# A graph layer with seven relations on one core: second batch's order by hand, first layer norm by halves, the turn of the sums moved, the last c products grouped

## The chip, the cores and the metric

One NeuronCore of a Trainium2 chip. The metric is the device time of one launch in microseconds. Beside TensorE (PE, matrix products) the core has VectorE (DVE), ScalarE (ACT) and GpSimd (POOL) for work on elements, and SyncE (SP), whose queue issues the DMA transfers. Each engine runs its own instructions in order; semaphores tie them together.

## What is computed

Sixteen graphs of 512 nodes with 128 features; `adj` is a full 512 x 512 f32 matrix of each. Cut to what matters:

```python
def _L0_gnn_ref(features, A1, A2, W, W_edges, b):
    eye = jnp.zeros_like(A1) + jnp.eye(N, dtype=A1.dtype)
    shifted = jnp.roll(eye, 1, axis=0)              # the roll is over the batch axis
    A_fwd = [A1, A2, shifted]
    A_list = A_fwd + [jnp.swapaxes(a, 1, 2) for a in A_fwd]
    A_list.append(eye)
    A = jnp.stack(A_list, axis=0)
    HW = jnp.einsum('bnf,rfo->rbno', features, W[:, :F]) \
        + jnp.einsum('rd,rdo->ro', W_edges, W[:, F:])[:, None, None, :]
    AHW = jnp.einsum('rbnm,rbmo->rbno', A, HW)
    return jnp.max(AHW, axis=0) + b

h = jnp.maximum(_layernorm(x, axis=-1), 0.0)
x = x + _L0_gnn_ref(h, adj, adj, L0_gnn_W, L0_gnn_W_edges, L0_gnn_b)
```

So there are seven products of which three are with h itself (relations 2, 5, 6), two with adjT h (3, 4) and two with adj h (0, 1). The constant c_r of a relation (from W_edges) is added plainly in the first three and times the row or column sum of adj in the other four.

## The kernel before

**Tiles.** Everything is kept turned, features on the partitions and nodes along the free axis, so each result is a 128 x 512 tile in one of the eight PSUM banks. `adj` and `adjT` of a batch come as two 1 MB transfers into one of two buffers each. Products are made in fp32r from a high and a low part: `hi*hi + hi*lo + lo*hi`, three matmuls for one. Of the four 128-row chunks of adj, one (WHOLE) is multiplied in f32 and three (SPLIT) from `a_hi` (ScalarE) and `a_lo` (two chunks by VectorE, the last one by GpSimd); the same for adjT with `aT_hi` and `aT_lo`.

**Stages of a batch b on TensorE**, one after the other (L809 to L819):

- `aggregate_T(b)`: h times adj into bank_gT (L704 to L716),
- `turn_h(b)`: four transposes of h into bank_p1 (L671),
- `turn_sums(b)`: four small matmuls that turn the row and column sums of adj, split into `sum_parts` by GpSimd, into bank_p2 (L679),
- `aggregate(b)`: h times adjT into bank_g (L725 to L736),
- products 0 to 2 with hT (L761 to L763), then `begin_products`: the sums times c into the banks of products 3 to 6 (L751), then products 3 to 6 with gT and g.

**The other engines.** ScalarE makes `a_hi`, `aT_hi` with the sums as their accumulators (`split_adj`, `split_adjT`, L389 to L405), h from x with the scale and shift of the layer norm (`make_h`, L418), the high parts of hT, gT and g, `sumsT` (L446), and the first of the seven maxima (`begin_best`, L453). VectorE does the layer norm's statistics (`variance`, L510 to L517, then `scale_and_shift`, L526 to L528), the low parts (`a_lo` L535, `aT_lo` L542, `h_lo` L548, hT, gT, g), and six maxima `take_best(b, 1..6)` (L576, L579) straight from PSUM. GpSimd makes the last chunks of `a_lo` and `aT_lo`, `sum_parts`, `x_bias` = x + b (L307), and the final sum into `o_sb` (L315).

**What sets the order.** Every engine's queue is written out by hand, a start for batch 0 and a loop over the rest; there is no scheduler. VectorE works ahead: in batch b it does the statistics of batch b+2 and shift and `a_lo` of batch b+1. An instruction that waits holds all behind it on its engine. These waits matter below: `aggregate(b)` writes bank_g, which product 6 of the batch before filled, so it waits for `best_done` of all six maxima of batch b-1 (`pe.wait_ge(best_done, b * NBEST)`); product 2 uses bank_p2, so it waits for `sumsT_ready`; `variance(b)` waits for x of batch b to land (`x_in`); GpSimd's `split_adj_last(b + 1)` waits for `h_lo`. The sync queue issues x, adj, adjT, W, bias and xT in one fixed order (L249 on); its load of adj b+2 waits for `gT_psum` and `a_lo` of batch b.

**The start.** Ten warm-up matmuls, then the turn of h of batch 0, for which x comes in two halves whose statistics are made as one group, then the aggregations of batch 0 in f32, chunk by chunk as the quarters of adj and adjT land.

## Time and profile before

| | before |
|---|---|
| timed runs, median (lowest to highest) | 216.88 us (216.61 to 218.16) |
| profiled execution, its time | 216.98 us |
| profiled execution, its span | 215.3 us |
| TensorE busy | 206.3 us, 96% of the span |
| VectorE, ScalarE, GpSimd busy | 177.0, 160.8, 95.9 us |
| DMA moved | 47.14 MB, mean 219 GB/s |
| mean granted TensorE clock | 0.989 |

The span runs from the first to the last instruction in the trace, the time of an execution also holds what lies around it. All times in the views count from the span's start. "PEclk" is the share of full TensorE clock that was granted. A timeline row reads: start, duration, engine, line of the kernel, operation, out<-in, shapes, how many were merged; in brackets the engine's idle time before it and what ended it.

### The profile page before, as it was taken

To read this page: it belongs to the slowest core of one execution; us is meant where nothing else is said; L and a number is where in the kernel's file an instruction comes from. 1 tells how busy PE (TensorE), PEld (TensorE's weight loads), DVE (VectorE), ACT (ScalarE), POOL (GpSimd) and SP (SyncE) were. 2 spreads that over 40 slices of the span, in tenths; PEclk is the share of its full clock that TensorE was granted. 3 is DMA by queue.
4 is the path that set the end of the run, shared out by engine and by line. 5 is a ranking of instruction groups with operands and counts; after the bars stand their busy time and mean duration, and the time that the engine had idled before them with its cause. 6 is when DMAs were issued, how large, how long until landed. Compare 5 with 4: busy or idle time off the path is not lost.

```text
span 215.3 us, 3420 instructions
## 1 busy us (share of the span) xinstructions
PE 206.3 (96%) x902; PEld 149.5 (69%) x902; DVE 177.0 (82%) x414; ACT 160.8 (75%) x431; POOL 95.9 (45%) x140
## 2 busy tenths in 40 slices
PE   7799779999999999999999999999999999999994
PEld 7456456777767777777767777776777777777772
DVE  3574997988889797988989798888979798888755
ACT  3779788697896969698796969689696969876220
POOL 3112946446172735527082644617273552718200
PEclk9999979999999999999999999999999999999998
DMA  5999995376693939678492938769393938610101
GB/s 175 313 345 370 376 362 199 108 292 245 202 336 93 380 79 313 215 253 283 156 355 69 374 127 295 241 198 335 86 384 89 342 130 253 234 53 0 50 0 49
DMA packets 31587, 47.14 MB, mean 219 GB/s; under 512 B 1632, under 2 KB 11088, under 8 KB 31568
## 3 DMA queue, kind: packets, MB, share of 16 engines
q1 hardware_dynamic: 31568, 46.92, 64.3%
q8 instruction: 7, 0.11, 0.2%
q14 instruction: 12, 0.10, 0.1%
HBM read 42.72 MB, written 4.19 MB: 218 GB/s over the span
## 4 chain that ended last, share of the span: by engine, by line
PE 84%; SPq 6%; DMA 5%; DVE 2%; issue 1%; ACT 1%; POOL 0%; DVEq 0%; ACTq 0%; POOLq 0%
PE bank_p L761 11%; PE bank_p L763 10%; PE bank_p L762 9%; PE bank_g L725 6%; PE bank_gT L704 6%; PE bank_g L730 5%; PE bank_g L729 5%; PE bank_g L736 5%; DMA adj_sb<-in_adj_dram 5%; PE bank_gT L716 5%; PE bank_gT L710 5%; PE bank_gT L709 4%; PE bank_p L751 3%; PE bank_p L679 3%; PE bank_p L671 3%; PE bank_g L762 2%
## 5 line engine op out<-in xcount | busy, mean ns | idle before, releaser
L321 POOL TENSOR_TENSOR a_lo<-adj_sb,a_hi 128x512 fp32r<-128x512 f32 x15 | 19.4, 1295 | 72.3 <-DVE h_lo L548 68.5
L579 DVE TENSOR_TENSOR best<-bank_p,best 128x512 f32<-128x512 f32 x48 | 33.2, 691 | 8.4 <-PE bank_p L763 7.3
L434 ACT ACTIVATE gT_hi<-bank_gT 128x512 fp32r<-128x512 f32 x16 | 9.6, 598 | 30.9 <-PE bank_gT L716 30.5
L576 DVE SCALAR_TENSOR_TENSOR best<-bank_p,c_col,best 128x512 f32<-128x512 f32 x32 | 24.0, 750 | 5.8 <-ACT best L453 5.1
L389 ACT ACTIVATE a_hi<-adj_sb 128x512 fp32r<-128x512 f32 x45 | 27.7, 620 | 1.3 <-DMA adj_sb<-in_adj_dram 1.3
L402 ACT ACTIVATE aT_hi<-adjT_sb 128x512 fp32r<-128x512 f32 x45 | 27.7, 620 | 0.0
L315 POOL TENSOR_TENSOR o_sb<-best,x_bias 128x512 f32<-128x512 f32 x15 | 20.0, 1332 | 15.8 <-DVE best L579 15.8
L418 ACT ACTIVATE h<-x_sb,shift,rstd 128x128 f32<-128x128 f32 x60 | 24.7, 497 | 1.4 <-DVE shift L528 1.4
L542 DVE TENSOR_TENSOR aT_lo<-adjT_sb,aT_hi 128x512 fp32r<-128x512 f32 x30 | 24.5, 854 | 0.0
L729 PE MATMUL bank_g<-aT_hi,h_hi 128*128 128x512 f32 x45 | 24.4, 541 | 0.0
L709 PE MATMUL bank_gT<-a_hi,h_hi 128*128 128x512 f32 x45 | 23.6, 525 | 0.0
L327 POOL TENSOR_TENSOR aT_lo<-adjT_sb,aT_hi 128x512 fp32r<-128x512 f32 x15 | 20.0, 1330 | 3.9 <-ACT aT_hi L402 3.9
L307 POOL TENSOR_TENSOR x_bias<-xT_sb,bias_sb 128x512 f32<-128x512 f32 x16 | 21.1, 1318 | 0.0
L535 DVE TENSOR_TENSOR a_lo<-adj_sb,a_hi 128x512 fp32r<-128x512 f32 x30 | 20.5, 724 | 0.0
L761 PE MATMUL bank_p<-hT_hi,w_hi 128*128 128x512 f32 x48 | 19.7, 410 | 0.0
L763 PE MATMUL bank_p<-hT_lo,w_hi 128*128 128x512 f32 x48 | 19.0, 395 | 0.0
L762 PE MATMUL bank_p<-hT_hi,w_lo 128*128 128x512 f32 x48 | 18.9, 393 | 0.0
L730 PE MATMUL bank_g<-aT_hi,h_lo 128*128 128x512 f32 x45 | 18.4, 409 | 0.0
L710 PE MATMUL bank_gT<-a_hi,h_lo 128*128 128x512 f32 x45 | 17.7, 393 | 0.0
L725 PE MATMUL bank_g<-adjT_sb,h 128*128 128x512 f32 x30 | 16.1, 620 | 0.0
L563 DVE TENSOR_TENSOR g_lo<-bank_g,g_hi 128x512 fp32r<-128x512 f32 x16 | 11.1, 691 | 5.7 <-ACT g_hi L440 5.7
L704 PE MATMUL bank_gT<-adj_sb,h 128*128 128x512 f32 x30 | 15.4, 595 | 0.0
(110 smaller groups left out, 501.8 us busy)
## 6 DMA issues: line engine op xcount, KB each, us to landing
adj_sb<-in_adj_dram SPq DMA_DIRECT2D x15, 1024.0 KB, 5.6
adjT_sb<-in_adjT_dram SPq DMA_DIRECT2D x15, 1024.0 KB, 5.6
xT_sb<-in_xT_dram SPq DMA_DIRECT2D x16, 256.0 KB, 5.9
x_sb<-in_x_dram SPq DMA_DIRECT2D x15, 256.0 KB, 6.1
out_dram<-o_sb SPq DMA_DIRECT2D x15, 256.0 KB, 5.9
adj_sb<-in_adj_dram SPq DMA_DIRECT2D x4, 256.0 KB, 3.4
adjT_sb<-in_adjT_dram SPq DMA_DIRECT2D x4, 256.0 KB, 4.8
...
```

The lines of the kernel that those rows point to most:

```text
L389: nc.scalar.activation(a_hi[q][:, i, :], adj_sb[q][:, c, :], ACT.Copy, accum_out=sums[q][:, 0, c:c + 1]).then_inc(ahi_ready, 1)
L402: nc.scalar.activation(aT_hi[q][:, i, :], adjT_sb[q][:, c, :], ACT.Copy, accum_out=sums[q][:, 1, c:c + 1]).then_inc(aThi_ready, 1)
L579: op = nc.vector.tensor_tensor(best[q][:, :], product, best[q][:, :], ALU.max)
L704: nc.tensor.matmul(bank_gT[:, 0:N], h[q][:, c, :], adj_sb[q][:, c, :], start=(c == WHOLE[0]), stop=False)
L709: nc.tensor.matmul(bank_gT[:, 0:N], h_hi[q][:, i, :], a_hi[q][:, i, :], start=False, stop=False)
L710: nc.tensor.matmul(bank_gT[:, 0:N], h_lo[q][:, i, :], a_hi[q][:, i, :], start=False, stop=False)
L725: nc.tensor.matmul(bank_g[:, 0:N], h[q][:, c, :], adjT_sb[q][:, c, :], start=(c == WHOLE[0]), stop=False)
L729: nc.tensor.matmul(bank_g[:, 0:N], h_hi[q][:, i, :], aT_hi[q][:, i, :], start=False, stop=False)
L730: nc.tensor.matmul(bank_g[:, 0:N], h_lo[q][:, i, :], aT_hi[q][:, i, :], start=False, stop=False)
L761: nc.tensor.matmul(dst, w_hi[:, i, :], hi[:, nodes], start=start, stop=False)
L762: nc.tensor.matmul(dst, w_lo[:, i, :], hi[:, nodes], start=False, stop=False)
L763: return nc.tensor.matmul(dst, w_hi[:, i, :], lo[:, nodes], start=False, stop=stop)
```

## The change

It has six parts: (1) x of batch 0 in two halves through two queues, with statistics, scale and shift made for each half, h's last quarter on VectorE instead of its second half, nine warm-up matmuls instead of ten, and `aggregate_T` ahead of `turn_h` in batch 0; (2) batch 0's and batch 1's order on VectorE and ScalarE written out; (3) `turn_sums` behind `aggregate` in each batch (behind products 3 and 4 in batch 0), with `copy_sumsT` behind `split_g`; (4) on VectorE `a_lo` of the next batch behind hT's low part; (5) `part_sums(b + 1)` at the end of GpSimd's batch instead of at the start of the next, and ahead of other work for batch 1; adj and adjT of batch 2 ahead of xT of batch 1 in the sync queue; (6) the c products of the last two half products made with those of products 3 to 5, the second half now going to bank_p0.

```diff
-WARM_UP = 10
+WARM_UP = 9
-        last_banks = (bank_g, bank_p[1])
+        last_banks = (bank_g, bank_p[0])
@@ sync
-            for i in range(2):
-                half = slice(i * HALF, (i + 1) * HALF)
-                sp.dma_start(x_sb[0][:, half, :], x_dram[0][:, half, :]).then_inc(x0_in[i], 16)
+            sp.dma_start(x_sb[0][:, :HALF, :], x_dram[0][:, :HALF, :]).then_inc(x0_in[0], 16)
...
             load_xT(0)
+            load_adj(2)
+            load_adjT(2)
             load_xT(1)
-            for b in range(B):
+            load_x(3)
+            for b in range(1, B):
+                if b + 1 < B:
+                    load_xT(b + 1)
                 if b + 3 < B:
                     load_x(b + 3)
                 if b + 2 < B:
                     load_adj(b + 2)
-                if b > 0:
-                    store(b - 1)
+                store(b - 1)
                 if b + 2 < B:
                     load_adjT(b + 2)
-                    load_xT(b + 2)
@@ gpsimd
             add_bias(0)
+            part_sums(1)
             split_adjT_last(1)
+            finish(0)
             add_bias(1)
             for b in range(1, B):
-                part_sums(b)
-                finish(b - 1)
+                if b >= 2:
+                    finish(b - 1)
                 if b + 1 < B:
...
                     split_adjT_last(b + 1)
+                    part_sums(b + 1)
@@ scalar
+            act.dma_start(x_sb[0][:, HALF:, :], x_dram[0][:, HALF:, :]).then_inc(x0_in[1], 16)
...
-            split_hT(0)
...
             split_gT(0)
+            split_hT(0)
...
             split_adj(1)
+            std_of(2)
             split_adjT(1)
-            std_of(2)
             for b in range(1, B):
-                if b + 1 < B:
+                if 2 <= b < B - 1:
                     split_adj(b + 1)
                 split_gT(b)
                 split_hT(b)
-                copy_sumsT(b)
                 if b + 1 < B:
                     make_h(b + 1)
                 split_g(b)
+                copy_sumsT(b)
                 begin_best(b)
+                if b == 1:
+                    split_adj(b + 1)
@@ vector
-            variance(0)
-            scale_and_shift(0)
+            first_variance(0, half_stats_done, half_aggr_done)
+            first_scale_and_shift(0, half_std_ready, half_rstd_ready, half_shift_ready)
+            first_variance(1, stats_done, aggr_done)
+            first_scale_and_shift(1, std_ready, rstd_ready, shift_ready)
...
             split_g_lo(0)
-            take_best(0, 1)
             split_h_lo(1)
             variance(2)
+            take_best(0, 1)
+            split_adj_lo(1)
             take_best(0, 2)
-            split_adj_lo(1)
+            scale_and_shift(2)
             for i in range(NH, NPROD):
                 take_best(0, i)
+            split_adjT_lo(1)
+            split_gT_lo(1)
+            split_hT_lo(1)
+            variance(3)
+            split_h_lo(2)
+            split_g_lo(1)
+            take_best(1, 1)
+            take_best(1, 2)
+            split_adj_lo(2)
+            for i in range(NH, NPROD):
+                take_best(1, i)
-            for b in range(1, B):
+            for b in range(2, B):
...
                     scale_and_shift(b + 1)
-                    split_adj_lo(b + 1)
                 split_gT_lo(b)
                 split_hT_lo(b)
                 if b + 1 < B:
+                    split_adj_lo(b + 1)
                     split_h_lo(b + 1)
@@ tensor, begin_products
+                if b == B - 1:
+                    pe.wait_ge(best_begun, B)
+                    for nodes, to in zip(HALVES, last_banks):
+                        add_sums(NPROD - 1, to, nodes, start=True)
@@ tensor, order
                 product(0, 0)
                 product(0, 1)
-                turn_sums(0)
...
                 passes(4, bank_of[4][:, 0:N], start=True)
+                turn_sums(0)
...
+            aggregate_T_first()
             turn_h(0)
-            aggregate_T_first()
...
                 turn_h(b)
+                aggregate(b)
                 turn_sums(b)
-                aggregate(b)
...
-            pe.wait_ge(best_done, (B - 1) * NBEST + 1)
             for nodes, to in zip(HALVES, last_banks):
-                add_sums(NPROD - 1, to, nodes, start=True)
                 product(B - 1, NPROD - 1, nodes, to)
```

`aggregate_T_first` now waits chunk by chunk for h's quarters (`half_h_ready`, `h_ready`, `h0_ready`). `first_variance(i)` and `first_scale_and_shift(i)` are `variance` and `scale_and_shift` for half i of batch 0.

Where instructions move, first on VectorE, behind `g_lo` of batch 0. Before (stats is `variance(2)`, its x is that of batch 2; the lone `best` rows are maxima 1 and 2 of batch 0, the rows of three and one are maxima 3 to 6):

```order
L563 TENSOR_TENSOR g_lo<-bank_g,g_hi 128x512
L576 SCALAR_TENSOR_TENSOR best<-bank_p,c_col,best 128x512
L548 TENSOR_TENSOR h_lo<-h,h_hi 128x384
L510 BN_STATS stats<-x_sb 128x6 x4
L515 MEMSET wait_carrier 128x1
L517 BN_AGGR mean_var<-stats 128x2 x4
L576 SCALAR_TENSOR_TENSOR best<-bank_p,c_col,best 128x512
L535 TENSOR_TENSOR a_lo<-adj_sb,a_hi 128x512 x2
L579 TENSOR_TENSOR best<-bank_p,best 128x512 x3
L579 TENSOR_TENSOR best<-bank_g,best 128x512
```

The same place in the changed kernel:

```order
L603 TENSOR_TENSOR g_lo<-bank_g,g_hi 128x512
L588 TENSOR_TENSOR h_lo<-h,h_hi 128x384
L532 BN_STATS stats<-x_sb 128x6 x4
L537 MEMSET wait_carrier 128x1
L539 BN_AGGR mean_var<-stats 128x2 x4
L616 SCALAR_TENSOR_TENSOR best<-bank_p,c_col,best 128x512
L575 TENSOR_TENSOR a_lo<-adj_sb,a_hi 128x512 x2
L616 SCALAR_TENSOR_TENSOR best<-bank_p,c_col,best 128x512
L566 RECIPROCAL rstd<-std 128x4
L568 SCALAR_TENSOR_TENSOR shift<-mean_var,rstd 128x4
L619 TENSOR_TENSOR best<-bank_p,best 128x512 x3
L619 TENSOR_TENSOR best<-bank_g,best 128x512
```

Both maxima now stand behind the statistics of batch 2, and scale and shift of batch 2 ahead of the last four.

Second, ScalarE from the end of batch 0's `sumsT` on, before (`a_hi` is adj of batch 2, in the first rows; `std` that of batch 2):

```order
L377 ACTIVATE std<-mean_var,eps 128x4
L389 ACTIVATE a_hi,sums<-adj_sb 128x512 x3
L392 ACTIVATE summed,sums<-adj_sb 128x512
L434 ACTIVATE gT_hi<-bank_gT 128x512
L428 ACTIVATE hT_hi<-bank_p 128x512
L446 ACTIVATE sumsT<-bank_p 128x512
L418 ACTIVATE h<-x_sb,shift,rstd 128x128 x4
L422 ACTIVATE h_hi<-h 128x384
L440 ACTIVATE g_hi<-bank_g 128x512
L453 ACTIVATE best<-bank_p,c_col 128x512
L402 ACTIVATE aT_hi,sums<-adjT_sb 128x512 x3
```

The same stretch, batch 1, in the changed kernel, behind `split_adjT(1)`:

```order
L444 ACTIVATE gT_hi<-bank_gT 128x512
L438 ACTIVATE hT_hi<-bank_p 128x512
L428 ACTIVATE h<-x_sb,shift,rstd 128x128 x4
L432 ACTIVATE h_hi<-h 128x384
L450 ACTIVATE g_hi<-bank_g 128x512
L456 ACTIVATE sumsT<-bank_p 128x512
L463 ACTIVATE best<-bank_p,c_col 128x512
L399 ACTIVATE a_hi,sums<-adj_sb 128x512 x3
L402 ACTIVATE summed,sums<-adj_sb 128x512
L412 ACTIVATE aT_hi,sums<-adjT_sb 128x512 x3
```

The splitting of adj of batch 2 has gone from the head of batch 1 to behind its first maximum, and `sumsT` to behind g.

## Rows read from the trace of the kernel before

**Rows 1.** Timeline of TensorE, batch 1 and the start of batch 2.
```profile
25.45 0.60 PE L671 MATMUL bank_p<-ident,h 128*128 128x128 f32 x4
28.07 0.66 PE L679 MATMUL bank_p<-ident_r,sum_parts 128*128 128x128 f32 x4 [2.02 <-POOL sum_parts L298]
28.57 1.11 PE L725 MATMUL bank_g<-adjT_sb,h 128*128 128x512 f32 x2
...
33.18 0.47 PE L761 MATMUL bank_p<-hT_hi,w_hi 128*128 128x512 f32 x1
...
38.78 1.02 PE L704 MATMUL bank_gT<-adj_sb,h 128*128 128x512 f32 x2
```
**Rows 2.** Timeline of TensorE, batch 3.
```profile
51.05 1.02 PE L704 MATMUL bank_gT<-adj_sb,h 128*128 128x512 f32 x2
...
54.34 0.64 PE L679 MATMUL bank_p<-ident_r,sum_parts 128*128 128x128 f32 x4
54.82 1.07 PE L725 MATMUL bank_g<-adjT_sb,h 128*128 128x512 f32 x2
...
57.82 0.40 PE L761 MATMUL bank_p<-hT_hi,w_hi 128*128 128x512 f32 x1
```
**Rows 3.** Timeline of TensorE, batch 0; the first row is the warm-up.
```profile
1.58 4.39 PE L799 MATMUL bank_p<-ident 128*128 128x128 f32 x20 [1.58 <-POOL ident L332]
7.07 0.63 PE L671 MATMUL bank_p<-ident,h 128*128 128x128 f32 x4 [1.09 <-DVE h L595]
7.53 3.60 PE L687 MATMUL bank_gT<-adj_sb,h 128*128 128x512 f32 x8
...
11.41 3.60 PE L694 MATMUL bank_g<-adjT_sb,h 128*128 128x512 f32 x8
...
16.88 0.66 PE L679 MATMUL bank_p<-ident_r,sum_parts 128*128 128x128 f32 x4 [0.47 <-POOL sum_parts L298]
...
18.83 0.48 PE L761 MATMUL bank_p<-hT_hi,w_hi 128*128 128x512 f32 x1
...
21.54 1.12 PE L704 MATMUL bank_gT<-adj_sb,h 128*128 128x512 f32 x2
```
**Rows 4.** Windows: stretch, busy times by engine, PEclk, DMA share, GB/s.
```profile
30.00:31.00 1.00, 1.00 (x4) 0.81 (x3) 0.97 (x4) 0.29 (x1) 0.00 (x0) 0.50 1.06 387
```
**Rows 5.** Timeline of VectorE.
```profile
3.02 0.49 DVE L510 BATCH_NORM_STATS2 stats<-x_sb 128x6 f32<-128x128 f32 x2 [1.09 <-DMA x_sb<-in_x_dram]
4.25 0.49 DVE L510 BATCH_NORM_STATS2 stats<-x_sb 128x6 f32<-128x128 f32 x2 [0.75 <-DMA x_sb<-in_x_dram]
...
5.99 0.60 DVE L591 TENSOR_SCALAR h<-x_sb,rstd,shift 128x128 f32<-128x128 f32 x2
...
20.50 0.86 DVE L510 BATCH_NORM_STATS2 stats<-x_sb 128x6 f32<-128x128 f32 x4
...
22.33 2.51 DVE L535 TENSOR_TENSOR a_lo<-adj_sb,a_hi 128x512 fp32r<-128x512 f32 x2
24.76 2.13 DVE L579 TENSOR_TENSOR best<-bank_p,best 128x512 f32<-128x512 f32 x3
...
30.60 1.28 DVE L535 TENSOR_TENSOR a_lo<-adj_sb,a_hi 128x512 fp32r<-128x512 f32 x2
```
**Rows 6.** DMA issues 6.7 to 7.1 us (KB each, us to landing); issued 6.60.
```profile
adjT_sb<-in_adjT_dram SPq DMA_DIRECT2D x1, 256.0 KB, 4.7
```
**Rows 7.** DMA issues 10.2 to 11.1 us: x of batch 2, issued 10.15.
```profile
x_sb<-in_x_dram SPq DMA_DIRECT2D x1, 256.0 KB, 9.9
```
**Rows 8.** The page's groups: busy us, mean ns of one.
```profile
L389 ACT ACTIVATE a_hi<-adj_sb 128x512 fp32r<-128x512 f32 x45 | 27.7, 620 | 1.3 <-DMA adj_sb<-in_adj_dram 1.3
```
**Rows 9.** Timeline of ScalarE, h of batch 2.
```profile
30.71 1.65 ACT L418 ACTIVATE h<-x_sb,shift,rstd 128x128 f32<-128x128 f32 x4 [0.98 <-DVE shift L528]
```
**Rows 10.** Timeline of VectorE, the end.
```profile
209.04 2.14 DVE L579 TENSOR_TENSOR best<-bank_p,best 128x512 f32<-128x512 f32 x3 [0.49 <-PE bank_p L763]
211.38 0.42 DVE L656 TENSOR_TENSOR best<-bank_g,best 128x256 f32<-128x256 f32 x1 [0.20 <-PE bank_g L763]
```

77 lines of the change are left out of this document (54 added, 23 removed).

## Prediction

> **What bounds the kernel now.** First the times: the profiled execution took 216.98 us for a span of 215.3 us, 1.68 more, and 0.10 over the median of the three timed runs (216.88), so I add differences to 216.98 and read the sum as the median too. Next TensorE's timeline once the pipeline is full: the aggregation of adj begins at 38.78 for batch 2 [rows 1] and at 51.05 for batch 3 [rows 2], 12.27 us apart, and thirteen batches run like that with no idle time on the engine. What isn't such a batch: the start (the same operation begins at 21.54 for batch 1 [rows 3]), batch 1 (21.54 to 38.78 = 17.24 us, 4.97 more than a full-speed batch), the last products, and whatever batch 2 can be made to wait for.
>
> Of the 4.97, TensorE stands 2.02 us after the turn of h (at 25.45) until GpSimd has `sum_parts` [rows 1]. Behind that gap the granted clock was 0.50, that is 1.2 instead of 2.4 GHz [rows 4], and the aggregation of adjT took 33.18 - 28.57 = 4.61 us [rows 1] where batch 3 takes 57.82 - 54.82 = 3.00 [rows 2]: 1.61 us for the clock. The rest, about 1.3, is mostly a wait for `a_lo` and its surroundings: the turn comes 25.45 - 21.54 = 3.91 after the batch's start, and in batch 3 the turn of the sums, which is one step later, comes after 3.29 [rows 2].
>
> **Step 1, the start: 1.2 us earlier at batch 1.** TensorE turns h at 7.07, 1.09 us after the warm-up, aggregates from 7.53, and comes to adjT at 11.41 [rows 3]. After the change the aggregation is first and needs only h's first quarter. The warm-up is one matmul (two passes of 4.39/20, 0.43 in all [rows 3]) shorter and ends near 5.5. h began at 5.99 with x's first half in at 3.02 [rows 5]; from this I take off the second half's wait of 0.75 and its statistics of 0.49: h's first half starts at 4.7 and the second, whose chain stands behind it, at 6.3, so the quarters are there at 5.2, 5.6, 6.8 and 6.9. Four steps of 0.86 (3.60/4, less the drain) lead to 8.9; turn 0.44; c products 0.44: adjT at 9.8. Its second quarter landed 4.7 us after its issue at 6.6 [rows 6], so at 11.3; x's second half moves to ScalarE's queue, every later issue of the sync queue comes up to 0.45 sooner, I take 10.9, and TensorE waits 0.3. Gain so far 11.41 - 9.8 - 0.3 = 1.3. Then the turn of the sums moves behind products 3 and 4, and nothing covers ScalarE's copy of `sumsT`: the turn's 0.66 [rows 3] and 0.6 for the copy stand before product 2, a gap near 0.8. Before, a gap of 0.47 stood ahead of the turn [rows 3]. Product 2 starts at 17.6 instead of 18.83; batch 1 begins 21.54 - 18.83 = 2.71 later: **20.3**, 1.2 earlier.
>
> **Step 2, the maxima of batch 0: the gain is lost on VectorE.** The aggregation of adjT of batch 1 writes bank_g, and waits for all six maxima of batch 0. Before, VectorE's queue led there so: variance of batch 2 at 20.50, a maximum, two `a_lo` at 22.33 (2.51 us), four maxima from 24.76, 0.71 each: 27.6 [rows 5]. Now that variance stands ahead of the first maximum too. It needs x of batch 2, issued at 10.15 and landed 9.9 us later [rows 7]: 20.05. For 0.25 MB that is the time of a full queue, and the same 5.0 MB lie ahead of it after the change; with the 0.45 of step 1 it lands at 19.6. VectorE has `h_lo` done at 17.2 and stands 2.4 us. From 19.6: variance 1.2, maximum 0.7, `a_lo` 2.45, maximum 0.7, the new reciprocal and shift 0.3, four maxima 2.85: **27.7**. The maxima end where they did, and TensorE, done with the turn of h at 25.1 (0.8 of that a wait for `a_lo`), waits 2.6 us for them. I keep the 2.51 of `a_lo`, since GpSimd's x_bias runs beside it in both; alone, the pair takes 1.28 [rows 5].
>
> **Step 3, to batch 2.** The 2.02 us wait for the sums is gone: they are turned after the aggregation, when they are long ready. adjT starts at 27.75 instead of 28.57, takes 3.0, the sums 0.45: 31.2, if the clock stays. The new gap is longer than the one that halved it, so I take the 1.6 again: 32.8 against 33.18. `hT_lo` is not in the way: variance, shift and `a_lo` for later batches, which stood in front of it, have moved, and it is done at about 31.3. Batch 2 begins 38.78 - 33.18 = 5.6 later: **38.4**, 0.4 earlier than before.
>
> **Step 4, batch 2: what was put off comes due.** ScalarE split adj of batch 2 while it waited in batch 1; now it does so after the first maximum, from 34.4, then adjT and adj of batch 3: 12 pieces of 0.62 [rows 8] and 0.3 for std: to 41.9. VectorE takes `a_lo` of batch 2 after two maxima, at 36.0, just when GpSimd gets its own piece, so I take the pair at 2.5 again: 38.5, four maxima to 41.3. TensorE reaches adjT of batch 2 at 38.4 + 3.4 = 41.8, no wait. Then VectorE: variance 1.2, `aT_lo` 1.5, shift 0.3: 44.3. ScalarE's h of batch 3 waits for this shift, and the new order puts g and the sums behind it: h 1.65 [rows 9] and 0.5 for h_hi, g and `sumsT` 0.55 each: 47.6. TensorE is at 41.8 + 3.0 + 0.45 = 45.25, waits 0.25 for `hT_lo`, and would begin product 2 at 46.9: it waits 0.7. Add 0.7 for that product and 3.4 to the next batch: **51.75** against 51.05, **0.7 later**.
>
> **Step 5, the other batches: nothing.** The turn of the sums leaves a place where it costs 0.48 from its start to the next operation's, 54.34 to 54.82 [rows 2], of which the switch of type is about 0.05 (the f32 pair behind it 1.07, behind products 1.02 [rows 2]), and gets one between products of one type. I put the difference at 0, bounds -0.05 and +0.05 per batch, 0.65 over thirteen. ScalarE then has `sumsT` ready 0.5 us ahead of product 2. The sync queue issues the same transfers in the same order from there on.
>
> **Step 6, the end: 0.1 us.** The c products of the last halves move forward. But VectorE takes the last whole maxima from 209.04 for 2.14 us and idles only 0.20 before the first half at 211.38 [rows 10]; that 0.20 is all there is, less what the two extra matmuls delay.
>
> **Sum.** 216.98 + 0.7 + 0 - 0.1 = 217.6; I predict **217.6 us**.
>
> Two rules speak to this. A pair of `a_lo` beside GpSimd took 2.51 us against 1.28 [rows 5]. The Trainium skill, "SBUF — State Buffer", section "SBUF: two separate sides", has it that the shared ports are held for a whole instruction and the loser fully blocks. By that rule both `a_lo` of batch 2 could each wait out a GpSimd operation, an estimated 1.1 us more than the row, and the time would be 218.7. The clock fell behind a gap of 2.02 us [rows 1, 4]. The Trainium skill, "TensorE: Matmul & The Clock Gate", section "HAM oscillation — how this bites in real kernels", worries only about longer gaps than any here; by it the clock would hold in batch 1, as in rival (a).
>
> **Rivals.** (a) The clock holds at 2.4 GHz in batch 1. Batch 2 begins at 36.9; the maxima of batch 1 end at 40.4, g and the sums follow at 46.8: batch 3 at 50.95, 216.8. Against it: the gap is longer than the one in [rows 1]. Chance 0.25. (b) VectorE is not held by x, which lands before 17.2. For it: only 0.25 MB. Against it: 20.05 measured. Everything behind comes 2.45 us sooner, TensorE's gap shrinks to 0.2, the clock holds: 216.8 - 2.45 = 214.4, the case on the faster side. Each us that x lands before 19.6 gives one. Chance 0.18. (c) The low clock lasts twice as long, as the gap is longer: adjT and the products of batch 1 lose 1.6 more, batch 2 begins at 40.0 and batch 3 at 52.3 and most of step 4's waits (0.9): 53.2, 219.1, slower by 1%. It decides if the clock is still low at the first product. Chance 0.12. (d) The sums' new place costs 0.05 to 0.1 a batch: 218.2 to 218.9. Chance 0.10. My forecast, give and take 0.7: 0.35.
>
> **Chances and range.** A measurement can tell about 1% here (2.2 us). Below 214.7 lie (b) and a little of (a): 0.20. Above 219.1 lie (c) and the edge of (d): 0.16. Same: 0.64. The range takes in (a), (d), the unknown costs of steps 2 to 5 and part of (b) and (c): 214.6 to 219.1.
>
> **What would show it.** Step 1: batch 1 begins at 20.3. Step 2: VectorE idle 2.4 us before the variance of batch 2, released by the DMA of x, and TensorE waiting some 2.6 us for a maximum ahead of adjT. Step 3: `sum_parts` gone from TensorE's waits, a low clock within 28 to 33. Step 4: new waits of TensorE in batch 2 for `hT_lo` and `sumsT`. Step 5: 12.27 per batch, no idle. It is wrong if x lands early, or if batch 2 runs through without a wait.

## The result, and the profile after

| | before | after |
|---|---|---|
| timed runs, median (lowest to highest) | 216.75 us (216.54 to 218.16) | 219.89 us (219.14 to 220.17) |
| ratio to before (95% interval) | | 1.0114 (1.0077 to 1.0151) |
| profiled execution, span | 215.3 us | 218.4 us |
| TensorE, VectorE busy | 206.3, 177.0 us | 207.1, 180.6 us |
| mean granted TensorE clock | 0.989 | 0.984 |

The changed kernel is 1.1% slower. The predicted time was 217.6 us; 219.89 lies above the range, 0.8 us above the nearest rival, (c) at 219.1. Of all the executions below one, of b2_early, took 512 us where its others took 217 to 219; no profile shows why, and it is left out. The timeline of TensorE of the changed kernel, from the warm-up to batch 3 (start, duration, what ran; in brackets the idle time ahead and what ended it):

```profile
5.58 4.68 PE L744 MATMUL bank_gT<-adj_sb,h 128*128 128x512 f32 x8
...
17.22 0.56 PE L730 MATMUL bank_p<-ident_r,sum_parts 128*128 128x128 f32 x4
18.46 0.50 PE L822 MATMUL bank_p<-hT_hi,w_hi 128*128 128x512 f32 x1 [0.69 <-ACT sumsT L456]
...
21.19 1.12 PE L761 MATMUL bank_gT<-adj_sb,h 128*128 128x512 f32 x2
...
25.11 0.60 PE L722 MATMUL bank_p<-ident,h 128*128 128x128 f32 x4
29.37 2.04 PE L782 MATMUL bank_g<-adjT_sb,h 128*128 128x512 f32 x2 [3.66 <-DVE best L619]
...
35.00 0.56 PE L730 MATMUL bank_p<-ident_r,sum_parts 128*128 128x128 f32 x4
35.39 0.45 PE L822 MATMUL bank_p<-hT_hi,w_hi 128*128 128x512 f32 x1
...
40.98 1.02 PE L761 MATMUL bank_gT<-adj_sb,h 128*128 128x512 f32 x2
...
47.29 0.56 PE L730 MATMUL bank_p<-ident_r,sum_parts 128*128 128x128 f32 x4
48.13 0.47 PE L822 MATMUL bank_p<-hT_hi,w_hi 128*128 128x512 f32 x1 [0.29 <-issue]
...
49.37 0.40 PE L824 MATMUL bank_p<-hT_lo,w_hi 128*128 128x512 f32 x1
50.10 0.50 PE L822 MATMUL bank_p<-hT_hi,w_hi 128*128 128x512 f32 x1 [0.33 <-ACT sumsT L456]
...
54.33 1.02 PE L761 MATMUL bank_gT<-adj_sb,h 128*128 128x512 f32 x2
```

Against [rows 1, 2, 3]: batch 1 begins 0.35 us earlier (21.19 for 21.54), the aggregation of adjT 0.80 later (29.37 for 28.57), the first product 2.21 later (35.39 for 33.18), batch 2 2.20 later (40.98 for 38.78), batch 3 3.28 later (54.33 for 51.05). From there to the end of the span it is 164.1 us after and 164.2 before: the whole loss lies between 25 and 54 us. It has two parts: batch 2 begins 2.2 us late, and batch 2 itself lasts 1.1 us longer (13.35 for 12.27). In batch 1 a wait of 3.66 us for VectorE's last maximum of batch 0 has taken the place of the 2.02 us wait for the sums. VectorE's timeline says what made it late:

```profile
19.58 0.88 DVE L532 BATCH_NORM_STATS2 stats<-x_sb 128x6 f32<-128x128 f32 x4 [1.68 <-DMA x_sb<-in_x_dram]
...
20.79 0.72 DVE L616 SCALAR_TENSOR_TENSOR best<-bank_p,c_col,best 128x512 f32<-128x512 f32 x1
21.43 3.06 DVE L575 TENSOR_TENSOR a_lo<-adj_sb,a_hi 128x512 fp32r<-128x512 f32 x2
24.41 0.74 DVE L616 SCALAR_TENSOR_TENSOR best<-bank_p,c_col,best 128x512 f32<-128x512 f32 x1
25.07 0.16 DVE L566 RECIPROCAL rstd<-std 128x4 f32<-128x4 f32 x1
25.27 1.18 DVE L568 SCALAR_TENSOR_TENSOR shift<-mean_var,rstd 128x4 f32<-128x4 f32 x1
26.37 2.13 DVE L619 TENSOR_TENSOR best<-bank_p,best 128x512 f32<-128x512 f32 x3
28.54 0.69 DVE L619 TENSOR_TENSOR best<-bank_g,best 128x512 f32<-128x512 f32 x1
```

and GpSimd's, in the same stretch:

```profile
20.96 1.28 POOL L328 TENSOR_TENSOR a_lo<-adj_sb,a_hi 128x512 fp32r<-128x512 f32 x1 [4.93 <-ACT a_hi L399]
22.19 1.74 POOL L314 TENSOR_TENSOR x_bias<-xT_sb,bias_sb 128x512 f32<-128x512 f32 x1
...
25.17 1.26 POOL L334 TENSOR_TENSOR aT_lo<-adjT_sb,aT_hi 128x512 fp32r<-128x512 f32 x1
```

x of batch 2 releases VectorE at 19.58. Then the pair of `a_lo` takes 3.06 us beside two operations of GpSimd (22.33 and 2.51 us in [rows 5]), and the shift, four numbers a partition, 1.18: it begins at 25.27, 0.10 behind GpSimd's `aT_lo`, and ends at 26.45, when that one ends (26.43). At 46.67, where GpSimd has nothing between 45.40 and 49.78, the same operation takes 0.16. The last maximum ends at 29.23. Behind the gap the clock is low; in the windows view (stretch, busy time of PE, PEld, DVE, ACT and POOL, granted clock, DMA share, GB/s) of the changed kernel:

```profile
27.00:28.00 1.00, 0.00 (x0) 0.00 (x0) 0.93 (x3) 1.00 (x3) 0.00 (x0) 1.00 1.11 330
28.00:35.00 7.00, 5.63 (x11) 3.81 (x12) 6.26 (x16) 0.66 (x2) 3.27 (x2) 0.51 0.56 197
35.00:36.00 1.00, 1.00 (x8) 0.91 (x7) 0.17 (x1) 0.80 (x2) 0.00 (x0) 1.00 0.00 0
```

The granted clock was 0.50 from 28.10 to 34.93, where before it was so from 29.48 to 32.90: the aggregation of adjT and the sums take 35.39 - 29.37 = 6.02 us.

### The profile page after: what moved, and what is told of

Same layout as the page of the kernel before. It is cut to its first block, busy times and chain, and to the rows that moved or that the text cites. A ratio compares the mean times of both kernels' runs of the same rounds, so it can differ in the third digit from the quotient of the medians.

```text
span 218.4 us, 3423 instructions
## 1 busy us (share of the span) xinstructions
PE 207.1 (95%) x900; PEld 150.2 (69%) x900; DVE 180.6 (83%) x416; ACT 161.1 (74%) x433; POOL 97.0 (44%) x140
## 4 chain that ended last, share of the span: by engine, by line
PE 86%; DVE 8%; issue 3%; ACT 1%; POOL 0%; DVEq 0%; POOLq 0%; ACTq 0%
PE bank_p L822 11%; PE bank_p L824 9%; PE bank_p L823 9%; PE bank_g L782 6%; PE bank_gT L761 5%; PE bank_g L787 5%; PE bank_g L786 5%; PE bank_g L793 5%; PE bank_gT L773 4%; PE bank_gT L767 4%; PE bank_gT L766 4%; DVE best L619 3%; PE bank_p L812 3%; PE bank_p L722 3%; PE bank_p L730 3%
## 5 line engine op out<-in xcount | busy, mean ns | idle before, releaser
L328 POOL TENSOR_TENSOR a_lo<-adj_sb,a_hi 128x512 fp32r<-128x512 f32 x15 | 19.6, 1305 | 69.0 <-DVE h_lo L588 57.7
L444 ACT ACTIVATE gT_hi<-bank_gT 128x512 fp32r<-128x512 f32 x16 | 9.5, 596 | 30.5 <-PE bank_gT L773 29.5
L322 POOL TENSOR_TENSOR o_sb<-best,x_bias 128x512 f32<-128x512 f32 x15 | 20.3, 1352 | 17.5 <-DVE best L619 17.5
L399 ACT ACTIVATE a_hi<-adj_sb 128x512 fp32r<-128x512 f32 x45 | 27.7, 621 | 0.0
L412 ACT ACTIVATE aT_hi<-adjT_sb 128x512 fp32r<-128x512 f32 x45 | 27.7, 621 | 0.0
L582 DVE TENSOR_TENSOR aT_lo<-adjT_sb,aT_hi 128x512 fp32r<-128x512 f32 x30 | 25.3, 884 | 0.0
L334 POOL TENSOR_TENSOR aT_lo<-adjT_sb,aT_hi 128x512 fp32r<-128x512 f32 x15 | 19.5, 1298 | 8.9 <-ACT aT_hi L412 8.9
L575 DVE TENSOR_TENSOR a_lo<-adj_sb,a_hi 128x512 fp32r<-128x512 f32 x30 | 22.1, 780 | 0.0
L314 POOL TENSOR_TENSOR x_bias<-xT_sb,bias_sb 128x512 f32<-128x512 f32 x16 | 22.0, 1377 | 0.0
L822 PE MATMUL bank_p<-hT_hi,w_hi 128*128 128x512 f32 x48 | 20.5, 427 | 1.3 <-ACT sumsT L456 1.0
L450 ACT ACTIVATE g_hi<-bank_g 128x512 fp32r<-128x512 f32 x16 | 9.6, 598 | 11.8 <-PE bank_g L793 11.2
L603 DVE TENSOR_TENSOR g_lo<-bank_g,g_hi 128x512 fp32r<-128x512 f32 x16 | 11.1, 691 | 6.4 <-ACT g_hi L450 6.4
```

Source lines behind the costliest of these rows:

```text
L399: nc.scalar.activation(a_hi[q][:, i, :], adj_sb[q][:, c, :], ACT.Copy, accum_out=sums[q][:, 0, c:c + 1]).then_inc(ahi_ready, 1)
L412: nc.scalar.activation(aT_hi[q][:, i, :], adjT_sb[q][:, c, :], ACT.Copy, accum_out=sums[q][:, 1, c:c + 1]).then_inc(aThi_ready, 1)
L582: nc.vector.tensor_tensor(aT_lo[q][:, i, :], adjT_sb[q][:, c, :], aT_hi[q][:, i, :].bitcast(F32), ALU.subtract).then_inc(aTlo_ready, 1)
L822: nc.tensor.matmul(dst, w_hi[:, i, :], hi[:, nodes], start=start, stop=False)
```

## The experiments

Each ratio is to the kernel before, timed beside it on the same chip; not all of them ran on the same chip, so kernels are compared by their ratios. The places are those of one profiled execution each ("maxima": end of the last maximum of batch 0; "adjT": start of that aggregation in batch 1; "product": the first product of batch 1; "low clock": the stretch at 0.50 in batch 1):

| kernel | ratio (95%) | batch 1 | maxima | adjT | product | batch 2 | batch 3 | low clock |
|---|---|---|---|---|---|---|---|---|
| before | 1 | 21.54 | 27.61 | 28.57 | 33.18 | 38.78 | 51.05 | 29.5-32.9 |
| after | 1.0114 | 21.19 | 29.23 | 29.37 | 35.39 | 40.98 | 54.33 | 28.1-34.9 |
| shift_late | 1.0048 (1.0019-1.0076) | 20.97 | 27.91 | 28.05 | 32.88 | 38.50 | 52.17 | none |
| x_late | 0.9963 (0.9932-0.9994) | 20.94 | 24.28 | 24.43 | 30.48 | 37.59 | 50.67 | 31.1-34.5 |
| filled | 1.0029 (1.0008-1.0049) | 20.68 | 28.79 | 28.93 | 32.38 | 38.00 | 51.64 | none |
| start | 0.9962 (0.9939-0.9986) | 20.19 | 26.85 | 27.81 | 32.42 | 38.03 | 50.32 | 28.4-31.8 |
| sums_late | 1.0017 (0.9986-1.0047) | 21.61 | 28.04 | 28.18 | 34.41 | 40.00 | 52.31 | 27.3-34.2 |
| tail | 1.0006 (0.9977-1.0036) | 20.96 | 27.56 | 28.93 | 34.27 | 39.79 | 52.06 | 27.1-33.9 |
| order_only | 1.0068 (1.0031-1.0104) | 20.90 | 29.00 | 29.14 | 33.74 | 39.26 | 52.09 | 30.0-33.4 |
| sums_back | 1.0050 (1.0027-1.0073) | 20.74 | 29.34 | 29.49 | 34.67 | 40.19 | 53.02 | 27.3-34.1 |
| start_back | 1.0128 (1.0089-1.0166) | 20.84 | 30.07 | 30.22 | 36.35 | 41.94 | 55.30 | 29.2-36.0 |
| b2_early | 1.0033 (1.0001-1.0066) | 20.81 | 28.84 | 28.99 | 33.99 | 39.57 | 51.84 | 29.7-33.1 |
| x_later | 0.9899 (0.9864-0.9935) | 20.87 | 24.22 | 24.37 | 27.76 | 38.20 | 50.49 | 32.5-35.9 |
| x_best | 0.9860 (0.9829-0.9891) | 20.97 | 24.30 | 24.45 | 27.86 | 33.56 | 48.41 | none |

The theories for batch 1: A, the work put in front of the maxima of batch 0 (variance, which waits for x, and shift); B, waits for the ports that VectorE shares with GpSimd; C, the low clock.

**x_late and shift_late** take work out of the front of the maxima.

```diff
@@ x_late, VectorE (and std_of(2) behind split_adjT(1) on ScalarE)
-            variance(2)
             take_best(0, 1)
             split_adj_lo(1)
             take_best(0, 2)
-            scale_and_shift(2)
             for i in range(NH, NPROD):
                 take_best(0, i)
+            variance(2)
             split_adjT_lo(1)
+            scale_and_shift(2)
@@ shift_late, VectorE
-            scale_and_shift(2)
             for i in range(NH, NPROD):
                 take_best(0, i)
+            scale_and_shift(2)
             split_adjT_lo(1)
```

> The changed kernel with one part of the second batch's order taken back: the statistics of batch 2 (which wait for its x to land) stand behind all six maxima of batch 0 on VectorE, scale and shift of batch 2 behind the low parts of adjT of batch 1, and ScalarE's std of batch 2 behind the split of adjT. Theory A (the wait for x in front of the maxima is the cause): the last maximum of batch 0 ends at 25.0 to 25.8 us instead of 29.2, TensorE's wait ahead of adjT of batch 1 shrinks from 3.66 us to under 1, the clock is not halved there, batch 2 begins at 34.5 to 36 instead of 40.98, and the time is 215 to 216.5. Theory B (it is the sharing of ports with GpSimd that makes the maxima late): they end at 27.5 or later, the time is 218 to 219. Theory C (the halved clock comes from the start's other phase, not from the gap): the clock is low in batch 1 in spite of the small gap.

> The changed kernel with scale and shift of batch 2 (1.38 us in its trace, 1.18 of it the shift beside GpSimd's low part of adjT) behind the four last maxima of batch 0 instead of ahead of them. Theory B (ports shared with GpSimd): the maxima end at 27.8 to 27.9 instead of 29.23, the shift takes 0.16 to 0.3 there, TensorE's wait ahead of adjT is 2.3 us, and the time falls by 0.7 to 1.4, to 218.5 to 219.2. Theory A: VectorE still stands 1.7 us for x, and the clock is low in batch 1 all the same, so the rest of the loss stays. If the shift only gets its wait elsewhere (GpSimd's final sum starts then), the time stays at 219.9.

Measured: 216.44 us and 218.01 us. In x_late the variance and the scale and shift are both gone from the front. The maxima end 4.95 us earlier (24.28) and no gap stands ahead of adjT; the time falls by 1.5% of before's, from slower to faster. Of the 4.95, 2.0 is the earlier first maximum (18.76 for 20.79), 1.8 the pair of `a_lo`, which now runs ahead of GpSimd's own piece and takes 1.28 us, and 1.2 the reciprocal and shift. The time is as expected; the clock fell later in the batch all the same, and batch 2 began at 37.59, behind the 34.5 to 36 expected. TensorE's timeline of x_late shows what is late next:

```profile
24.43 1.10 PE L782 MATMUL bank_g<-adjT_sb,h 128*128 128x512 f32 x2
...
28.08 0.73 PE L793 MATMUL bank_g<-aT_lo,h_hi 128*128 128x512 f32 x2 [0.94 <-DVE aT_lo L582]
28.65 0.56 PE L730 MATMUL bank_p<-ident_r,sum_parts 128*128 128x128 f32 x4
30.48 0.47 PE L822 MATMUL bank_p<-hT_hi,w_hi 128*128 128x512 f32 x1 [1.27 <-issue]
```

The norm now stands ahead of `aT_lo` and `hT_lo`, which TensorE waits for. In shift_late the four-element shift alone is moved, and VectorE reads:

```profile
21.94 2.41 DVE L575 TENSOR_TENSOR a_lo<-adj_sb,a_hi 128x512 fp32r<-128x512 f32 x2
24.27 0.74 DVE L616 SCALAR_TENSOR_TENSOR best<-bank_p,c_col,best 128x512 f32<-128x512 f32 x1
25.04 2.14 DVE L619 TENSOR_TENSOR best<-bank_p,best 128x512 f32<-128x512 f32 x3
27.21 0.69 DVE L619 TENSOR_TENSOR best<-bank_g,best 128x512 f32<-128x512 f32 x1
27.82 0.17 DVE L566 RECIPROCAL rstd<-std 128x4 f32<-128x4 f32 x1
28.02 0.16 DVE L568 SCALAR_TENSOR_TENSOR shift<-mean_var,rstd 128x4 f32<-128x4 f32 x1
28.10 3.47 DVE L582 TENSOR_TENSOR aT_lo<-adjT_sb,aT_hi 128x512 fp32r<-128x512 f32 x2
```

The maxima end 1.3 us earlier and the shift takes 0.16 us. A and B both hold: the wait for x puts the maxima late, and beside GpSimd an operation that looks like nothing takes a microsecond more. Part of that microsecond comes back one operation later: the pair of `aT_lo` takes 3.47 us beside GpSimd's final sum and x_bias, where the changed kernel has 2.35, and TensorE waits for it:

```profile
31.63 0.73 PE L793 MATMUL bank_g<-aT_lo,h_hi 128*128 128x512 f32 x2 [0.87 <-DVE aT_lo L582]
```

The time fell by 1.4 us by the ratios, the upper end of the 0.7 to 1.4 expected. The profiled execution has no low clock, as three of its ten have none by their mean clocks (0.995 or more). The three with the long low stretch took 218.73 us in the median, where the three such of the changed kernel, on another chip, took 219.95: 1.2 us at like clocks.

**filled** asks what the clock costs. TensorE does 16 extra matmuls of the identity in the gap; their output is overwritten.

```diff
                 turn_h(b)
+                if b == 1:
+                    pe.wait_ge(best_begun, 1)
+                    for _ in range(FILL):
+                        nc.tensor.matmul(bank_p[0][:, 0:P], ident[:, :], ident[:, :], start=True, stop=True)
                 aggregate(b)
```

> The changed kernel with 16 matmuls of identity by identity (128 columns, f32, results not used) between the turn of h and the aggregation of adjT in batch 1, where TensorE otherwise stands 3.66 us: only the idle time is taken away, the maxima end when they did. Theory C' (the halved clock behind the gap costs time of its own): the clock stays full in batch 1, the aggregation of adjT takes 3.0 us instead of 5.6, batch 2 begins at 38.2 to 38.6 instead of 40.98; what then remains is set by VectorE and ScalarE in batch 2, so the time falls by 1 to 2.5 us, to 217.4 to 218.9. Rival (VectorE's and ScalarE's postponed work bounds batch 2 anyway): batch 2 begins earlier but batch 3 at the same 54.3, the time stays within 0.4 of 219.9.

Measured: 217.65 us, 2.2 less than the changed kernel. The timeline, and the window:

```profile
25.05 3.74 PE L877 MATMUL bank_p<-ident 128*128 128x128 f32 x32
28.93 1.10 PE L783 MATMUL bank_g<-adjT_sb,h 128*128 128x512 f32 x2
...
24.00:35.00 11.00, 10.81 (x66) 8.81 (x66) 10.82 (x23) 5.99 (x13) 5.21 (x7) 1.00 0.82 282
```

adjT and the sums take 32.38 - 28.93 = 3.45 us at full clock against 6.02: 2.57 us for the clock, and the two profiled executions differ by 2.66 (217.51 and 220.17). The medians differ by 2.2 us and the ratios by 1.8; one of the four executions of the changed kernel had a shorter low stretch (mean clock 0.992, 219.14 us). Batch 2 lasts 13.64 us in filled, for 13.35: 0.3 is given back there.

**start, sums_late, tail, order_only** each add one part of the change to the kernel before; order_only has the order of VectorE, ScalarE, GpSimd and the loads behind the start.

```diff
@@ sums_late (ScalarE's copy_sumsT behind split_g)
                 turn_h(b)
-                turn_sums(b)
                 aggregate(b)
+                turn_sums(b)
@@ tail
-        last_banks = (bank_g, bank_p[1])
+        last_banks = (bank_g, bank_p[0])
```

> The kernel before with only the first part of the change: x of batch 0 through two queues, layer norm by halves, nine warm-up matmuls, the aggregation of adj ahead of the turn of h, and batch 0's front order on ScalarE and VectorE up to the low part of g; all else as before. Theory: batch 1 begins 0.3 to 1.2 us earlier than 21.54, and this is lost at the maxima of batch 0, which hang on a_lo of batch 1 and end at 27 to 27.6, so the time is that of the kernel before within 0.5 us, 216.3 to 217.2. Rival D (the start itself is what slows the changed kernel, since its first aggregation runs at 1.2 GHz and the gap behind it grows): 217.5 or more. Rival E (the start's gain is kept): 215.6.

> The kernel before with one part of the change alone: from batch 1 on TensorE turns the sums behind the aggregation of adjT, and ScalarE copies the turned sums behind the high part of g. Theory A, the place is free in the steady batches (the trace of the changed kernel has 12.28 us from batch to batch, before 12.27 to 12.31) and saves what batch 1 waits for the sums: the gap of 2.02 us that begins at 26.05 ends when bank_g is free at 27.6 instead of 28.07, adjT(1) begins at about 27.75 instead of 28.57, time 216.0 us, ratio 0.994 to 0.999. Theory B, the sums' copy is late for the first product in every batch (the first product waits .3 to .4 us): .05 to .1 us a batch, 217 to 218 us, ratio above 1.001. Granted clock: one low stretch near 3.4 us about 30 us as before.

> The kernel before with the last part of the change alone: the sums' matmuls of the last two c products stand ahead with the others, and the last product's second half goes to the first bank. Theory A: the end is set by the last products' own matmuls, then one maximum of each half, the addition and the store; nothing but the order of 2 short matmuls changes: 0 to -0.2 us, ratio 0.999 to 1.000. Theory B: at the end TensorE waits for a bank to be free ahead of the last products, and this wait falls away: -0.5 to -1.0 us, ratio 0.995 to 0.998. Theory C: the first bank is free later than the second, +0.2 to +0.5 us.

> The kernel before with only the order of the changed kernel behind the start: VectorE from the low part of g of batch 0 on, ScalarE from adj of batch 1 on, GpSimd, and the loads' queue; the start, the place of the turned sums and the end stay as before. Theory A (the loss lies in this order, ahead of adjT(1) and in batch 2): variance(2) waits for x in front of the maxima, these end at 29 us or later instead of 27.6, adjT(1) begins at 29.3 to 30, batch 2 lasts 13 us or more instead of 12.27; with the start 0.3 to 0.8 later than in the changed kernel the time is 219.5 to 220.5 us, ratio 1.012 to 1.018. Theory B (the loss comes from the start's or the sums' part, or from how they meet this order): 216.5 to 218 us, ratio below 1.006.

Measured: 216.19, 217.49, 217.14 and 218.32 us. The start alone gains 0.4%, a little more than expected (maxima at 26.85, expected 27 to 27.6); the sums' new place and the end move nothing that can be told from no change, so neither theory on the sums is decided by the time (adjT at 28.18 for 27.75, and a low stretch of 6.8 us for 3.4); the order loses 0.7%. Adding 0.9962, 1.0017, 1.0006 and 1.0068 gives 1.0053, half of what the whole lost, so the parts seem to meet; the intervals of the four, 0.5 to 0.7% wide, leave room for some of the difference. order_only missed both expectations (ratio 1.0068 between them), but its trace has theory A's marks: maxima at 29.00, adjT at 29.14, batch 2 12.83 us long.

**sums_back, start_back, b2_early** take one thing out of the changed kernel. The first puts the turn of the sums ahead of the aggregation again, the second brings back the old start, the third does batch 2's adj early:

```diff
@@ b2_early, ScalarE, batch 1
                     make_h(b + 1)
+                if b == 1:
+                    split_adj(b + 1)
                 split_g(b)
                 ...
                 begin_best(b)
-                if b == 1:
-                    split_adj(b + 1)
@@ VectorE
             split_hT_lo(1)
+            split_adj_lo(2)
+            split_h_lo(2)
             variance(3)
-            split_h_lo(2)
             split_g_lo(1)
             take_best(1, 1)
             take_best(1, 2)
-            split_adj_lo(2)
```

> The changed kernel with one part undone: from batch 1 on the sums are turned ahead of the aggregation of adjT again, and their copy stands behind the high part of hT. What the parts gave alone, start .83 faster, sums .37 slower (interval from .3 faster to 1.0 slower), end 0, order 1.48 slower, makes +1.0 us; the whole was +2.5 (219.89 against 217.4 by its ratio 1.0114). Theory A, the turned sums meet the late batch 2 (stalls of .29 and .33 us there) and the long low clock: without this part batch 2 lasts 12.8 us as in order_only instead of 13.35 and the time is 218.3 to 219.0, ratio 1.005 to 1.008. Theory B, the place of the sums is free here too and the rest is the start's meeting with the order: ratio 1.009 to 1.013, batch 2 13.2 us or more.

> The changed kernel with one part undone: the start as before (layer norm of batch 0 in one, turn of h ahead of the first aggregation, 10 warm-ups), order of batches 1 and 2, sums and end as changed. Theory A, the low stretch that lasts 6.8 us where it was 3.4 comes with the changed start (the first transfers, norm and aggregation end earlier while VectorE's wait for x of batch 2 ends at the same 19.6, so the gap grows from 3.3 to 3.66 us): here mean clocks near .99, the time is that of order_only plus the sums' .2 to .5, ratio 1.007 to 1.010. Theory B, it comes with the turned sums behind the gap (TensorE has less to do ahead of it): clocks of .984 in most runs as in the changed kernel, ratio 1.012 to 1.017. In both adjT(1) begins at 29.3 us or later, for the wait for x is not the start's.

> The changed kernel, where ScalarE splits adj of batch 2 in the 6.5 us in which it idles ahead of the high part of g of batch 1 (28.7 to 35.2 us), and VectorE makes its low part behind that of hT of batch 1 and not among the maxima of batch 1. Theory A, the longer batch 2 (13.35 instead of 12.28 us) comes of this postponed work alone: maxima of batch 1 end 1.3 to 2.4 us earlier against the start of batch 2, batch 2 lasts 12.3 to 12.5, the rest stays (adjT(1) at 29.3, product(1,0) at 35.4 with a long low stretch): ratio 1.0114 less .004 to .005, so 1.006 to 1.008. Theory B, batch 2 is longer for another reason (the ports shared with GpSimd, the turned sums): batch 2 13.0 us or more, ratio 1.010 to 1.013.

Measured: 218.30, 219.86 and 218.02 us. sums_back went by its theory A, at the lower end of its range: 1.4 us less than the changed kernel by the ratios, although adding the part to the kernel before had cost nothing measurable. Its timeline of TensorE:

```profile
25.15 0.60 PE L722 MATMUL bank_p<-ident,h 128*128 128x128 f32 x4
25.50 0.64 PE L730 MATMUL bank_p<-ident_r,sum_parts 128*128 128x128 f32 x4
29.49 2.04 PE L782 MATMUL bank_g<-adjT_sb,h 128*128 128x512 f32 x2 [3.34 <-DVE best L619]
```

The sums' parts are ready at 25.5 by GpSimd's new order, and the turn lies inside the gap, free; behind the aggregation it stands on the path. From adjT to the first product is 5.18 us here and 6.02 in the changed kernel, batch 2 lasts 12.83 us and 13.35: 1.36 us together. start_back answers the start's question: 1.0128, no faster clock without the new start (0.984 in four of six executions); its theory A falls and its theory B has the time. Its x landed late too (VectorE starts the variance at 21.05), so one profile does not say what the start is worth there. b2_early shows the cause of the long batch 2: it lasts 51.84 - 39.57 = 12.27 us, with no wait of TensorE in it, less than the 12.3 to 12.5 of its theory A. ScalarE had stood idle just there; the changed kernel's timeline of ScalarE:

```profile
28.16 0.52 ACT L432 ACTIVATE h_hi<-h 128x384 fp32r<-128x384 f32 x1
35.20 0.60 ACT L450 ACTIVATE g_hi<-bank_g 128x512 fp32r<-128x512 f32 x1 [6.51 <-PE bank_g L793]
```

Its ratio is 0.008 lower, 1.8 us, more than expected, where batch 2 explains 1.07. The profiled execution had the short low stretch and six of the ten others the long one, so the clock explains little of the other 0.7; it is within the intervals of the two ratios and stays open.

**x_later and x_best** move what was late in each run before it. x_later puts the norm of batch 2 behind all low parts of batch 1 and splits adj of batch 2 early; x_best brings g, the sums and the first maximum of batch 1 ahead of h of batch 2 (variance and shift of batch 2 are gone from the front of the maxima as in x_late, and variance(4) stands behind `hT_lo` of batch 2):

```diff
@@ x_best against the changed kernel, VectorE, from the maxima of batch 0 on
             split_adjT_lo(1)
             split_gT_lo(1)
             split_hT_lo(1)
-            variance(3)
-            split_h_lo(2)
+            variance(2)
             split_g_lo(1)
+            scale_and_shift(2)
+            split_adj_lo(2)
             take_best(1, 1)
             take_best(1, 2)
-            split_adj_lo(2)
+            split_h_lo(2)
             for i in range(NH, NPROD):
                 take_best(1, i)
+            variance(3)
@@ ScalarE, batch 1
                 split_gT(b)
                 split_hT(b)
-                make_h(b + 1)
+                split_adj(b + 1)
+                std_of(2)
                 split_g(b)
                 copy_sumsT(b)
                 begin_best(b)
-                split_adj(b + 1)
+                make_h(b + 1)
```

> The changed kernel with the norm of batch 2 (variance, scale and shift) behind all low parts of batch 1 on VectorE, and adj of batch 2 split by ScalarE in the stretch in which it idled (28.2 to 35.2 us), its low part by VectorE right behind. If the losses are what the runs so far say (work put ahead of the maxima of batch 0; low parts of adjT and h late behind the norm, .94 and 1.27 us in the run x_late; adj(2)'s low part among the maxima of batch 1, which lengthens batch 2 by .8 to 1.1 us): adjT(1) at 24.4 with no gap, the first product of batch 1 at 27.8 to 28.3, batch 2 at 33.5 to 34.5, batch 3 12.3 to 12.6 later, time 212 to 214 us, ratio 0.978 to 0.988. Rival: the stream of transfers is the next limit (the 16 DMA engines are 80 to 100% busy from 2 to 33 us): adj of batch 2 or x of batch 3 lands late, batch 2 begins at 36 or later and the time is 215.5 to 216.5 us, no better than x_late (216.44).

> The run x_later with what its trace showed late put right: there TensorE waited 3.11 us at 29.37 for the turned sums, which ScalarE copied behind h of batch 2, which waited for scale and shift, and these had a turn of the ports behind GpSimd (shift 1.25 us); now the high part of g, the turned sums and the first of the maxima of batch 1 stand ahead of h of batch 2 on ScalarE, the low part of g ahead of scale and shift on VectorE, variance(3) behind the maxima of batch 1, variance(4) behind the low parts of batch 2. If that is the whole of it: product(1,0) at 27.8 as there, no gap above .5 us behind it, batch 2 at 33.5 to 34.5, time 211 to 213 us, ratio 0.970 to 0.981. Rival: the maxima and low parts are then late by the same amount (VectorE has the work of batches 1 and 2 in less time) or transfers land late: batch 2 or 3 is longer by 2 to 3 us and the time is 214.5 to 215.5 us, as x_later (215.18).

Measured: 215.18 us and 213.96 us (213.91 to 214.28). x_later got adjT at 24.37 and the first product at 27.76 as expected, and then 3.11 us of waiting, so it missed its 212 to 214 us. Its rival had the late batch 2 (38.20) for another reason, late transfers:

```profile
27.37 0.56 PE L733 MATMUL bank_p<-ident_r,sum_parts 128*128 128x128 f32 x4
...
32.48 0.79 PE L825 MATMUL bank_p<-hT_hi,w_hi 128*128 128x512 f32 x1 [3.11 <-ACT sumsT L456]
```

x_best has that gone: batch 2 begins at 33.56, 7.4 us before the changed kernel's, and batch 1 has no low clock. Part is given back in batch 2:

```profile
41.59 0.47 PE L829 MATMUL bank_p<-hT_hi,w_hi 128*128 128x512 f32 x1 [1.17 <-issue]
43.77 0.50 PE L829 MATMUL bank_p<-hT_hi,w_hi 128*128 128x512 f32 x1 [0.55 <-ACT sumsT L456]
45.08 0.50 PE L819 MATMUL bank_p<-sumsT,c_rows 32*128 32x512 f32 x3 [0.35 <-DVE g_lo L608]
```

ScalarE waits 2.43 us for the statistics of batch 3 (to 36.93) before it splits adj of batch 3, and `hT_hi` and `hT_lo` follow from that. So its expectation (211 to 213) was missed by 1 us and its rival (214.5 to 215.5) by 0.5. It is 1.4% faster than the kernel before and beats both.

## Why the prediction was wrong, step by step

**Step 1, start at 20.3: half right.** Measured 21.19. A slip comes first: 18.83 less the gain of 1.3, less the old gap of 0.47, plus the new one of 0.8 is 17.9 for product 2 and 20.6 for batch 1, not 17.6 and 20.3. In the run start, which keeps the turn of batch 0's sums where it was, batch 1 began at 20.19. The rest is the clock. The eight matmuls of the first aggregation took 4.68 us, not 3.6: the granted clock was full only from 7.62 us, where before it was from 5.59, and this varies from one execution to the next (4.49 to 7.62 in the profiles here). The wait for `sumsT` was 0.69, near the 0.8 that I had; in filled, with a full clock from 4.55, batch 1 began at 20.68. None of it moved the end, since VectorE's wait for x covered it.

**Step 2, maxima at 27.7: the step that failed.** The wait for x was right (19.58, forecast 19.6), the 1.68 of idle time was less than 2.4 since `h_lo` ended later. But the maxima ended at 29.23. From 19.6 I had 8.2 us of work, which is 27.8 and not 27.7; it took 9.65: the pair of `a_lo` 2.98 for 2.45, from its start to the next operation's, reciprocal and shift 1.30 for 0.3. Nothing was wrong in the order, two durations were, both of operations that run beside GpSimd.

The two are not of one kind. The shift took 1.18 to 1.25 us in all six kernels that have it there (after, filled, order_only, sums_back, start_back, b2_early): this 1.0 us is the term that I had wrong. The pair took 2.38 to 2.48 in the other five and in shift_late, as forecast. Only in the profile of the changed kernel did VectorE reach the pair (21.43) 0.8 us ahead of the end of GpSimd's `a_lo` (22.24); in the other six it was 0.1 to 0.2. So this half us belongs to one execution. In filled, which has the pair at 2.39, the maxima ended at 28.79.

The Trainium skill, "SBUF — State Buffer", section "SBUF: two separate sides", has it that the shared ports are held for a whole instruction and the loser fully blocks. The traces agree: wherever a GpSimd operation had started ahead of a shift, 23 times in the fourteen profiles, the shift ended 0.01 to 0.03 us behind the end of that operation. I had tried the rule only on `a_lo` of batch 2 and set it aside; that pair took 2.39 there (I had 2.5). It acted here, on the smallest operation in the queue, and shift_late has 0.16 for it. The sign of it was in the profile of the kernel before, where the shift of batch 1 stands beside a GpSimd operation that runs from 15.27 to 16.01:

```profile
15.31 0.72 DVE L528 SCALAR_TENSOR_TENSOR shift<-mean_var,rstd 128x4 f32<-128x4 f32 x1
```

**Step 3, low clock for 1.6 us: rival (c), mis-sized.** adjT and the sums took 6.02 us; I had 3.0 + 0.45 + 1.6 = 5.05. The low stretch was 6.8 us instead of 3.4, and 5.56 of it fell on work. Rival (c) tied its length to the length of the gap and was right on the length for a reason that does not hold: the kernel before and the run tail have the same code up to the last batch and the same gap (2.02 and 2.01 us), and the low stretch was 3.4 us in one and 6.8 in the other:

```profile
28.01 1.12 PE L679 MATMUL bank_p<-ident_r,sum_parts 128*128 128x128 f32 x4 [2.01 <-POOL sum_parts L298]
28.93 2.02 PE L725 MATMUL bank_g<-adjT_sb,h 128*128 128x512 f32 x2
```

The profiles show what goes with the length. In the five in which the clock fell while TensorE still stood in the gap of batch 1 (after, sums_late, tail, sums_back, start_back) the low stretch was 6.8 us; in the six in which it fell after TensorE had work again (before, x_late, start, order_only, b2_early, x_later) it was 3.4. What sets the moment of the fall is not shown; the mean clocks below say that it differs between executions of one kernel. By the profiles the long stretch alone gives a mean clock of 0.984 and the short one 0.992, and low clock at the very end takes off up to 0.005. Of 80 executions of the kernel before, 24 had 0.984 or less (217.9 us in the median), 43 had 0.987 to 0.992 (217.1) and 13 had 0.997 or more, which leaves no room for either (216.7); of the changed kernel 3 of 4 had the long stretch and one the short.

So rival (a), a clock that holds, did not come true in the changed kernel, and its chance of 0.25 was too high for this gap: none of the 40 executions of the five kernels with gaps of 3.3 to 3.7 us in their profiles (after, order_only, sums_back, start_back, b2_early) held it. Behind gaps of 1.7 to 2.5 us some did, by a mean of 0.995 or more: 13 of 80 of the kernel before, 4 of 10 of sums_late, 3 of 10 of shift_late, 1 of 12 of tail, none of 10 of start. The Trainium skill, "TensorE: Matmul & The Clock Gate", section "HAM oscillation — how this bites in real kernels", worries only about longer gaps than those in the kernel before; in 67 of its 80 executions, with a gap of 2.02 us in the profile, the clock fell all the same. I also booked the sums' new place as the gain of a removed wait. It was GpSimd's new order that removed it; the move itself took a turn out of a free gap (sums_back).

**Step 4, batch 2 at 13.35 us: right.** Forecast 51.75 - 38.4 = 13.35, measured 54.33 - 40.98 = 13.35, with waits for `hT_lo` and `sumsT` where I had them (13.35 is the steady 12.27 and 1.08). The timeline prints 0.29 and 0.33 us for them, counted from the modelled ends of the matmuls before. From start to start the two places take 0.84 and 0.73 us (47.29 to 48.13, 49.37 to 50.10) where b2_early has 0.39 and 0.23: 0.45 and 0.50, for my 0.25 and 0.7. The sum, 0.95, is as forecast; that the two errors cancel is luck. The rest, 0.1, is in the first matmul behind the second wait (0.34 to the next start, for 0.24).

**Steps 5 and 6: right.** From batch 3 to the end 0.1 us less than before; 12.28 a batch. One sum in step 4 is off without effect: 12 pieces of 0.62 and 0.3 behind 34.4 end at 42.1, not 41.9. Rival (d) fell for the steady batches. Rival (b), x early, fell; x_best gains 3.0 us by its ratio, near the 2.5 that (b) priced, but it moves VectorE's wait and much else instead of having x early.

The sum: adjT began at 29.37 where I had 27.75, 1.6 us, nearly all of it from the two durations on VectorE in step 2; the longer low clock of step 3 added 1.0. Together they are the 2.6 us between 217.6 and the profiled 220.17. Of that, the shift's 1.0 would come again in every execution; the pair's 0.5 and the clock's 1.0 depend on the execution. The executions of the changed kernel ran from 219.14 to 220.17 us, so even the fastest lay beside the upper end of my range, 219.1.
